# Turning the gate and up weights on VectorE instead of TensorE, in a NF4 feed-forward kernel with adapters

## The reference

```python
# layer 0: a 64x64 matrix chosen per sample, then a dense matrix with averaged LoRA adapters and a bias
y  = einsum('bct,bcd->bdt', x, L0_cond_weights[itok_B_0_15])
x1 = x + einsum('bsd,od->bso', y, W) + bias + lora(y)
# layer 1: a rank-16 adapter chosen per sample, then a gated feed-forward layer with NF4 weights
z    = einsum('bnr,bor->bno', einsum('bni,bri->bnr', x1, B[itok_B_3_7]), A[itok_B_3_7])
Wg   = NF4[gate_codes] * gate_scales   # (2752, 1024), one scale to 64 columns; Wu and Wd likewise
out  = x1 + einsum('bsi,hi->bsh', silu(z @ Wg.T) * (z @ Wu.T), Wd)
```

## Time and profile before

| | us |
|---|---|
| median of the runs | 1036.76 |
| profiled execution | 1037.4 |
| its span | 1035.5 |
| TensorE busy | 1005.8 (97%) |
| VectorE busy | 841.6 (81%) |
| ScalarE busy | 793.5 (77%) |
| GpSimd busy | 223.2 (22%) |

### The profile page before, as it was taken

One profiled execution on the slowest core, in us unless ns is written; L12 is line 12 of the kernel. 1 busy time (PEld: TensorE's weight loads), 2 busy tenths in 40 slices (PEclk: granted clock), 3 DMA queues, 4 the chain that ended last, 5 costly groups with the idle time before them and its releaser, 6 DMA issues.

```text
span 1035.5 us, 14607 instructions
## 1 busy us (share of the span) xinstructions
PE 1005.8 (97%) x5368; PEld 858.6 (83%) x5368; DVE 841.6 (81%) x834; ACT 793.5 (77%) x946; POOL 223.2 (22%) x269
## 2 busy tenths in 40 slices
PE   4999999999999899999999999999999999999998
PEld 3898898998898777788888888888888888888886
DVE  3999999989999889978887788887887879784344
ACT  4788887888888779888888888888887878884120
POOL 4014434324322301120111111111122112112000
PEclk9999999999999999999999999999999999999999
DMA  9844455446432436755654645655464545565666
GB/s 249 245 119 127 113 138 124 104 139 149 104 104 62 82 61 122 132 100 115 118 106 82 114 95 98 121 102 103 82 122 87 103 96 109 95 102 143 162 223 225
DMA packets 65397, 126.27 MB, mean 122 GB/s; under 512 B 6544, under 2 KB 38816, under 8 KB 65328
## 3 DMA queue, kind: packets, MB, share of 16 engines
q0 software_dynamic: 15200, 51.41, 31.9%
q1 hardware_dynamic: 48800, 72.88, 23.1%
q10 hardware_dynamic: 1328, 1.05, 0.3%
HBM read 66.61 MB, written 67.11 MB: 129 GB/s over the span
## 4 chain that ended last, share of the span: by engine, by line
PE 84%; DVE 9%; ACT 3%; issue 2%; DMA 1%; ACTq 0%; DVEq 0%
PE ps_z L1074 21%; PE ps_y L1074 21%; PE ps_z L948 13%; PE ps_gu L1053 11%; PE ps_t L982 5%; DVE val L735 4%; PE ps_t L990 3%; PE ps_gu L990 3%; DVE val L737 3%; PE ps_y L935 2%; PE ps_gu L965 2%; ACT ring L566 1%; PE ps_t L957 1%; DMA la<-in_L_ffn_lora_A 1%; DVE val L754 1%
## 5 line engine op out<-in xcount | busy, mean ns | idle before, releaser
L566 ACT ACTIVATE ring<-codes 128x1024 f32<-128x1024 int32 x455 | 452.6, 1051 | 17.9 <-DVE val L735 17.8
L735 DVE TENSOR_TENSOR val<-val,ring 128x1024 f32<-128x1024 f32 x260 | 320.6, 1233 | 36.3 <-ACT ring L566 20.4
L737 DVE SCALAR_TENSOR_TENSOR val<-ring,val 128x1024 f32<-128x1024 f32 x195 | 239.9, 1230 | 39.4 <-ACT ring L566 31.5
L539 POOL DMA_DIRECT2D out<-staged x80 | 68.8, 860 | 315.3 <-ACT staged L685 307.9
L866 DVE TENSOR_TENSOR inter<-ps_gu,inter 128x512 f32<-128x512 f32 x88 | 60.5, 687 | 74.5 <-ACT inter L671 74.5
L671 ACT ACTIVATE inter<-ps_gu 128x512 f32<-128x512 f32 x88 | 52.4, 595 | 71.8 <-PE ps_gu L1053 69.3
L948 PE MATMUL ps_z<-we_hi,y_hi 128*128 128x512 f32 x256 | 104.8, 409 | 0.5 <-DVE y_lo L785 0.5
L948 PE MATMUL ps_z<-we_hi,y_lo 128*128 128x512 f32 x256 | 100.4, 392 | 0.0
L948 PE MATMUL ps_z<-we_lo,y_hi 128*128 128x512 f32 x256 | 99.9, 390 | 0.0
L677 ACT ACTIVATE in_hi<-inter 128x512 fp32r<-128x512 f32 x88 | 55.4, 630 | 48.1 <-DVE inter L866 48.1
L481 POOL TENSOR_TENSOR st_hi<-ga_f,one 128x128 fp32r<-128x128 f32 x42 | 40.7, 968 | 218.1 <-ACT ga_f L606 218.1
(11 more groups left out here) (130 smaller groups left out, 1856.6 us busy)
## 6 DMA issues: line engine op xcount, KB each, us to landing
out<-staged POOLq DMA_DIRECT2D x80, 512.0 KB, 5.4
codes<-in_L_ffn_gate_codes SPq DMA_DIRECT2D x21, 512.0 KB, 4.9
codes<-in_L_ffn_up_codes SPq DMA_DIRECT2D x21, 512.0 KB, 4.2
codes<-in_L_ffn_down_codes SPq DMA_DIRECT2D x21, 512.0 KB, 4.0
xs<-in_x SPq DMA_DIRECT2D x16, 512.0 KB, 4.3
out<-in_L_ffn_bias SPq DMA_DIRECT2D x4, 2048.0 KB, 13.4
out<-xs POOLq DMA_DIRECT2D x16, 512.0 KB, 5.5
ring<-out SPq DMA_DIRECT2D x16, 512.0 KB, 4.6
```

The costliest lines, as they stand in the source:

```text
L539: pool.dma_start(out_rows[t * P:(t + 1) * P, :], staged[:, place, :], accum_op=ALU.add).then_inc(acc_out[place], 16)
L566: act.activation(ring[:, (k - 1) % RING, :], codes[:, n % 2, :], ACT.Identity, bias=offset, scale=slope).then_inc(lines, 1)
L735: ins = dve.tensor_tensor(v, v, line, pick)
L737: ins = dve.scalar_tensor_tensor(out=v, in0=line, scalar=add, in1=v, op0=ALU.add, op1=pick)
```

## The change

Gate, up and tail units are no longer turned by TensorE. Their codes are loaded in a quartered layout: four DMAs, one for each 32 partitions, bring a quarter of the columns (256) of all 128 rows, so that partition 32a + p holds, for i = 0 to 3, columns 256a to 256a + 255 of row 32i + p. After decoding and scaling, one VectorE instruction transposes the 32x32 blocks (128x1024 elements, read eight elements apart, written densely) into one of two `wt` buffers, which is then what it was before. It is a ninth step of a gate or up unit, so that there are 563 steps instead of 520.

The scales have to follow the layout: they are loaded raw and moved in setup by 32 small matmuls with slices of the identity into `ps_y` (`place_scales`) and two ScalarE copies. `cond_y` waits for these.

The ring has four buffers instead of five. Phase A has ten chunks of gate and up (22 units with the two down units) and 12 or 13 steps a tile; 9 steps lie in setup. The other two chunks go to phase B, whose groups have 6, 9, 9, 10 and 8 units in place of 6, 8, 8, 8 and 8. Gate and up units may be ready 0.3 slots ahead of their place instead of 0.8. `evac_wt` on ScalarE is gone.

```diff
-    RING = COMBOS - 2
+    RING = COMBOS - 3
-    UNITS = [(kind, c) for c in range(12) for kind in "gu"]
+    UNITS = [(kind, c) for c in range(10) for kind in "gu"]
...
-        [("d", 3), ("d", 4), ("d", 5), ("d", 6), ("g", 12), ("u", 12)],
-        [("d", 7), ("g", 13), ("d", 8), ("u", 13), ("d", 9), ("g", 14), ("d", 10), ("u", 14)],
-        [("d", 11), ("g", 15), ("d", 12), ("u", 15), ("d", 13), ("g", 16), ("d", 14), ("u", 16)],
-        [("d", 15), ("g", 17), ("u", 17), ("d", 16), ("g", 18), ("u", 18), ("d", 17), ("d", 18)],
+        [("d", 3), ("d", 4), ("g", 10), ("d", 5), ("u", 10), ("d", 6)],
+        [("d", 7), ("g", 11), ("d", 8), ("u", 11), ("g", 12), ("d", 9), ("u", 12), ("d", 10), ("g", 13)],
+        [("d", 11), ("u", 13), ("d", 12), ("g", 14), ("u", 14), ("d", 13), ("g", 15), ("d", 14), ("u", 15)],
+        [("d", 15), ("g", 16), ("u", 16), ("g", 17), ("u", 17), ("g", 18), ("d", 16), ("u", 18), ("d", 17), ("d", 18)],
...
-        if 5 * t % 8 < 5:
+        if t % 8 in (0, 3, 6):
             PLACE_A[t, 1] = len(PLACE_A)
...
-    STEPS = COMBOS + 1
-    STEPS_SETUP = 8
-    STEPS_A = [13] * NT
+    STEP = [(n, op) for n, (kind, _) in enumerate(UNITS) for op in range(1, COMBOS + (2 if kind == "d" else 3))]
+    STEPS_SETUP = 9
+    STEPS_A = [12 + (t % 4 == 0) for t in range(NT)]
...
-            then, due = max(place - AHEAD, 0.0), STEPS * (n + 1)
+            then, due = max(place - (0.3 if is_gu(n) else 0.8), 0.0), DONE[n + 1]
...
-                    sp.dma_start(codes[:, slot, :], src[c * P:(c + 1) * P, :]).then_inc(signal, 16)
+                    quarter = D // PQ
+                    for a in range(PQ):
+                        part = codes[a * SQ:(a + 1) * SQ, slot, :].rearrange("p (i j) -> p i j", i=PQ)
+                        cols = slice(a * quarter, (a + 1) * quarter)
...
+                            sp.dma_start(part, src[c * P:(c + 1) * P, cols].rearrange("(i p) j -> p i j", p=SQ)
+                                         ).then_inc(signal, 16)
...
                     act.wait_ge(codes_in[n % 2], CODE_COUNT[n])
-                    wait(act, turned, n - 2)
+                    if n >= 3:
+                        wait(act, *((gu_turned, GU_NO[n - 2]) if is_gu(n - 3) else (turned, D_NO[n - 2])))
...
-            def evac_wt(n):
-                m = GU_NO[n]
-                act.wait_ge(turned, n + 1)
-                wait(act, ga_mm, m)
-                act.activation(wt[:, :, :], ps_t[:, :].rearrange("p (q i) -> p q i", q=DC), ACT.Copy
-                               ).then_inc(evicted, 1)
...
+                if op == COMBOS + 2:
+                    m = GU_NO[n]
+                    dve.wait_ge(scaled, n + 1)
+                    wait(dve, ga_mm, m - 1)
+                    quarters = v.rearrange("p (i j q) -> p q i j", i=PQ, q=DC)
+                    dve.transpose(wt[:, m % 2, :, :].rearrange("p q (i j) -> p q i j", i=PQ), quarters).then_inc(gu_turned, 1)
+                    return
...
+            def place_scales():
+
+                pe.wait_ge(gu_scales_in, 16 * 4)
+                for kind, chunks in ((0, FULL + 1), (1, FULL)):
+                    to = ps_y[:, kind * HALF:kind * HALF + chunks * SB].rearrange("p (c i b) -> p i c b", i=PQ, b=SB // PQ)
+                    for a in range(PQ):
+                        for i in range(PQ):
+                            ins = pe.matmul(to[a * SQ:(a + 1) * SQ, i, :, :], ident[:, i * SQ:(i + 1) * SQ],
+                                            scales_raw[:, kind, 0:chunks, a * PQ:(a + 1) * PQ], start=i == 0, stop=i == PQ - 1)
+                ins.then_inc(scales_mm, 1)
+
             def turn_unit(n, x1_turns):
+                if UNITS[n][0] != "d":
+                    return
...
             def adapter_ga(n):
                 m = GU_NO[n]
-                pe.wait_ge(evicted, n + 1)
-                wait(pe, ga_evac, m - 1)
+                pe.wait_ge(gu_turned, m + 1)
+                wait(pe, ga_evac, m)
...
+                if jc == SCALES_JC - 1:
+                    place_scales()
```

More of the change, by code:

```diff
@@ L61, in adaln_ffn @@
     HALF = 512
+    SQ = 32
+    PQ = P // SQ
     NCOND = cond_w.shape[0]
@@ L121, in adaln_ffn, with lines_by @@
     D_NO = [sum(k == "d" for k, _ in UNITS[:n]) for n in range(NU + 1)]
-    CODE_COUNT = [16 * sum(1 + (UNITS[m][1] == TAIL) for m in range(n % 2, n + 1, 2)) for n in range(NU)]
+    PIECES = {"g": PQ, "u": PQ, "t": 2 * PQ, "d": 1}
+    CODE_COUNT = [16 * sum(2 if UNITS[m] == ("d", TAIL) else PIECES[UNITS[m][0]] for m in range(n % 2, n + 1, 2))
+                  for n in range(NU)]
     UNIT_OF = {unit: n for n, unit in enumerate(UNITS)}
     GROUP_OF = {c: g for g, chunks in enumerate(GROUPS) for c in chunks}
-    STEPS = COMBOS + 1
-    STEPS_SETUP = 8
-    STEPS_A = [13] * NT
-    LEAD = 2
-    LINES_AT = [STEPS_SETUP + LEAD + sum(STEPS_A[:t]) for t in range(NT + 1)]
+    STEP = [(n, op) for n, (kind, _) in enumerate(UNITS) for op in range(1, COMBOS + (2 if kind == "d" else 3))]
+    DONE = [sum(m < n for m, _ in STEP) for n in range(NU + 1)]
+    STEPS_SETUP = 9
+    STEPS_JC = [1] * (DC - 1) + [STEPS_SETUP - DC + 1]
+    STEPS_A = [12 + (t % 4 == 0) for t in range(NT)]
+    LEAD = 2
+    SCALES_JC = 3
+    def lines_by(steps):
+        if steps >= len(STEP):
+            return NLINES * NU
+        n, op = STEP[steps]
+        return min(NLINES * n + min(op - 1, NLINES) + LEAD, NLINES * NU)
+    STEPS_AT = [STEPS_SETUP + sum(STEPS_A[:t]) for t in range(NT + 1)]
     AHEAD = 0.8
     def steps_by(slot):
-        at, done = -1.0, LINES_AT[NT] - LEAD
+        at, done = -1.0, STEPS_AT[NT]
         for place, n in sorted(TURN_AT.items()):
@@ L174, in adaln_ffn @@
         lbq = sb("lbq", [P, DC, P], F32, setup)
+        scales_raw = sb("scales_raw", [P, 2, FULL + 1, SB], F32, setup)
         setup.close()
@@ L569, in some_lines @@
             def some_lines(first, count):
-                for j in range(first, first + count):
+                for j in range(lines_by(first), lines_by(first + count)):
                     line(j // NLINES, j % NLINES)
-            def evac_wt(n):
-                m = GU_NO[n]
-                act.wait_ge(turned, n + 1)
-                wait(act, ga_mm, m)
-                act.activation(wt[:, :, :], ps_t[:, :].rearrange("p (q i) -> p q i", q=DC), ACT.Copy
-                               ).then_inc(evicted, 1)
             def evac_wd(n):
                 c = UNITS[n][1]
-                act.wait_ge(turned, n + 1)
+                act.wait_ge(turned, D_NO[n] + 1)
                 if c >= WD:
@@ L629, in _ @@
                            ps_t[:, :].rearrange("j (q p) -> j q p", q=DC), ACT.Copy).then_inc(setup_evac, 1)
-            some_lines(0, 2)
-            at = 2
+            for j in range(lines_by(0)):
+                line(0, j)
+            at = 0
             for jc in range(DC):
-                some_lines(at, 1)
-                at += 1
+                some_lines(at, STEPS_JC[jc])
+                at += STEPS_JC[jc]
                 if jc == DC - 1:
@@ L712, in _ @@
                     some_lines(at, steps // 2)
-                    if before is not None and UNITS[before][0] != "d":
+                    if is_gu(before):
                         evac_ga(before)
@@ L742, in decode @@
                     if n == 0:
-                        dve.wait_ge(gu_scales_in, 16 * 4)
+                        dve.wait_ge(scales_ready, 1)
                     v = v.rearrange("p (b j) -> p b j", j=BLK)
-                    scales = gu_scales[:, c, "gu".find(kind) if kind != "t" else 0, :].unsqueeze(2).to_broadcast([P, SB, BLK])
+                    of = gu_scales[:, 1 if kind == "u" else 0, c, :, :].rearrange("p i b -> p (i b)")
+                    scales = of.unsqueeze(2).to_broadcast([P, SB, BLK])
                 elif c == TAIL:
```

67 lines of the change are left out of this document (39 added, 28 removed).

## The result

The changed kernel takes 1075.72 us in the median (1074.04 to 1079.36), the kernel before 1036.92 beside it: the ratio is 1.038, 95% interval 1.0365 to 1.0395. It is slower by 39 us, 14 us beyond the end of the range. Of the rivals, (b) has the sign and the cause, though its dear end, 1063, is 13 us short.

A forecast was written before the change was run, and what follows sets the result against it. The prediction took TensorE as the bound, VectorE just under it. Terms 5.5 - 21.4 - 1.6 - 1.6 + 4.8 + 2.6 + 12.9 - 4 = -2.8 gave 1034 us, 1033 with cheaper setup; range 1019 to 1062.

The forecast's parts named there:

- (b): Rival: the transpose's strided read is paid, T = 2.02 on 38 transposes, +30 us: 1063, or 1047 at T = 1.6; chance 0.30.
- T: Length of the new VectorE transpose, bounded between 1.22 and 2.02 us and taken as 1.23.
- Setup: Before phase A: 32 small fp32 matmuls that place the scales add 5.5 us, with nothing to hide them.
- Phase A to group 0: Phase A 21.4 us shorter with VectorE becoming the bound; start of phase B 1.6 shorter as the `wd_early_lo` wait goes.
- Group 0: First group of phase B: two turns less on TensorE, -1.6 us.
- Groups 1 and 2: Phase B: more VectorE steps, less shorter line waits and spare time of 6.6 and 8.8 us: +4.8 and +2.6.
- Group 3: Phase B: VectorE's added steps less spare time give +16.9 us; about 4 carried into group 4, leaving +12.9.
- Group 4: Phase B: five turns less on TensorE, and VectorE has room: -4 us.
- Loads: Gate/up loads as four issues instead of one cost nothing if ScalarE's eight lines, over 7 us, still cover them.
- Line waits stay: Phase B: VectorE's built-in waits for ScalarE's lines, 0.8 us each, stay: 8 to 10 of them in groups 1 to 3.
- Rival (a): TensorE stays the bound everywhere as line waits close up: -32 us at best, -20 with a third of VectorE's excess; chance 0.08.
- Rival (c): Four ring buffers instead of five make new steps in groups 1 to 3 find lines late: +10 us, 1043; chance 0.10.

The follow-up runs named there:

- the dense read: The changed kernel with the VectorE transpose reading whole 32-element runs instead of elements eight apart (output not the reference's): 1040.36 us, ratio 1.0034.
- e12_at_most_six: The changed kernel with dense transpose read, `ad` rows reordered in setup, LEAD 3 and at most 6 decode steps per phase B slot: 1021.85 us, ratio 0.9845.

## Why the prediction was wrong

The step that failed is the price T, taken as 1.23 us and measured as 2.16. The argument that a strided read is cheap came from TensorE's weight loads in the earlier trace rows, another engine. (Even there the step shows faintly: in phase B of the kernel before the eight loads of a gate or up unit take 1.08 us, those of a down unit, read densely, 1.02 or 1.03.) The row on VectorE itself, L812 at 2.02 us, was set aside because its write was strided. But it reads its second input, `lbt_hi`, with the same step of eight as it writes, so that it never spoke for a cheap read. The runs show that it doesn't matter on which side the distance stands, and 2.02 was the right row, a little low for 2.16.

The rule of the Trainium skill that was weighed against it ("Advanced Engine Details and Errata", SBUF Cachelines: a new 16-byte line at each access is penalised) agrees with the transposes: 1.24 at 8 bytes, 2.06 at 16, 2.11 at 32. The Trainium skill's other page, "Vector Engine (DVE) Microarchitecture Reference", section 3.8, gave the dense end, one element per cycle and lane; the dense blocks' 1.24 us for 1024 elements are what the other dense instructions of this size take (1.23 to 1.25), and no run here counts cycles.

Given T, the count of transposes works. Rival (b) counted 38 transposes on the path. 38 x (2.16 - 1.24) = 35.0; measured between the dense read and the changed kernel, 35.4. At T = 2.02 it gave 1063; at 2.16 it would have given 1033 + 38 x 0.93 = 1068. The last 7 us to 1075.7 are the terms below, since the dense read takes 1040.4 and not 1033. The same sum crosses the time of before at T = 1.33, sooner than the 1.4 that it was given; but with T measured at 1.24 the kernel is still slower than before (ratio 1.0034), not faster by 2.8 us.

The other steps are read from the dense read, whose T is the assumed one. Its profiled execution took 1038.5 where the sum gives 1034.6, its median 1040.4.

- **VectorE is a second bound just under TensorE**: right. Taking 24 us off TensorE's busy time (1005.8 to 981.9) gave nothing.
- **Setup** +5.5: +3.1 there, +4.0 in the changed kernel (+4.9 and +5.8 against the setup of 39.3 us, so whether anything but the placing lengthens it can't be told). The placing matmuls took 3.0 us, not 5.5, as the timeline of the changed kernel shows (start us, us):

```profile
24.85 3.06 PE L1011 MATMUL ps_y<-scales_raw,ident 128*32 128x88 f32 x64
27.84 1.09 PE L954 MATMUL ps_gu<-ident,w_stage 128*128 128x128 f32 x8
```

- **Phase A to group 0** -23.0: -21.5. The merges at 1.33 and the transposes at 1.14 together fit this stage; they weren't measured apart.
- **Group 0** -1.6: -5.6. The sum counted only the turns. TensorE also waited there for what turning needs, in the kernel before (364:465):

```profile
PE ps_y L1074 <- ACT staged L685: 2.2, 3, 1.1
PE ps_t L990 <- ACT wt L578: 1.7, 1, 1.7
```

  The second is gone with the copy to `wt`, of the first 1.2 are left in the dense read: 2.7 more, 4.3 with the turns. The other 1.3 stay open.
- **Groups 1 and 2** +4.8 and +2.6: +5.5 and +5.6. The forecast told the two apart only by their spare time, 6.6 and 8.8 us; they came out alike. Half of the 2.2 us between them was no spare time: before, VectorE was busy for 102.1 us in group 1 and 101.1 in group 2, in the dense read for 116.3 and 116.4. The rest stays open.
- **Group 3** +12.9: +18.8. This is the worst term after T. The 4 us to be carried into group 4 were not: TensorE stood still inside group 3, at the starts of its blocks, three times and up to 4.5 us each (4.4 in the row of the changed kernel above). Without the carry the sum gives +16.9. VectorE's busy time there grew by 28.5 us (101.6 to 130.1), where the sum has 29.4.
- **Group 4** -4: -4.6. **Loads** at nothing: nearly right. Each of the four issues lands in 3.8 us in the median, and ScalarE waits for codes twice in the whole changed kernel, 2.5 us in setup and 1.0 in phase A. That is a sign the forecast had named against itself, but a small one: VectorE waits for no line in phase A.
- **Line waits stay**: right as a description of the changed kernel (10, 10 and 11 of them), wrong as a judgement, since they hang on `LEAD`. Rival (a) says that they close when VectorE is late. They don't, but if they are made to go and the read is dense, its time comes near: 1022.6 against its 1012 to 1025. (Its second figure is off: with a third of VectorE's excess left, 29.6 / 3 = 9.9, its -32.4 becomes -22.5, so 1014 and not 1017.)
- **Rival (c)**: no sign of it. Line waits fell, and four buffers cost nothing in the kernel before; five in the changed kernel weren't tried.

## What to carry to other kernels

Price an access pattern on the engine that will run it, and take the nearest row of that engine, even if there the pattern stands on the output as well. Where one unmeasured price decides between faster and slower, as T did here, its dear end deserves as much weight as its cheap one. Choose the block order so that each read is dense, and put the permutation into a small operand that is prepared once. Before moving work to an engine that is nearly full, count what its producers' lead makes it wait: a wait that cost nothing while TensorE was the bound was worth 18 us where VectorE was.

## What the runs showed of the hardware

- VectorE, fp32, 128x1024: a 32x32 transpose takes 1.24 us densely or 8 bytes apart, 2.06 at 16 bytes, 2.11 to 2.18 at 32, on the input as on the output. A two-input product goes from 1.25 us densely to between 2.07 and 2.14 at 32 bytes, a copy from 0.72 to 1.19 reading so and 1.23 writing so; a multiply-add with constants that reads so takes 1.18 (it wasn't tried densely). Distances other than 32 bytes were tried for the transpose's input alone.
- TensorE's granted clock had no fall in the profiled execution of the kernel before (some others had a mean of 0.993). In the changed kernel it fell to half (1.2 GHz) nine times before the end, three times in the dense read, after TensorE had waited. The row at 535.53 above (under e12_at_most_six) shows one: pairs of matmuls last 1.09 and 1.05 us after 2.69 us of waiting, where such pairs lasted 0.62, and it lasts 3.4 us. By windows of the changed kernel (groups 2 and 3; TensorE, its loads, VectorE, ScalarE, GpSimd busy, then the clock, and the share and GB/s of the DMA engines):

```profile
594.00:727.00 133.00, 125.62 (x592) 103.99 (x591) 120.72 (x113) 105.75 (x130) 21.72 (x27) 0.97 0.54 99
727.00:876.00 149.00, 132.28 (x611) 107.33 (x610) 135.78 (x125) 114.82 (x140) 26.40 (x30) 0.95 0.49 93
```

  Eight falls last 3.4 us and one 6.8, 34 us in all, so TensorE lost at most 17 us to them, and 7 in the dense read. The difference of 10 us is a rival for a part of the 35.4. No run separated it, but little of it can lie on the path: in groups 1 to 3 of the changed kernel, where six of the nine falls are, VectorE waited 0, 1.3 and 0.4 us for the silu of TensorE's products.
